# Statistic sums once a round behind a branch, a store's two issues apart, and fourteen steps loaded at once, in a displaced 5x5 convolution kernel

## The reference

```python
def _gn(v, G=32, eps=1e-5):
    g = v.reshape(B_, G, C_ // G, H_, W_)
    return ((g - mean(g)) / jnp.sqrt(var(g) + eps)).reshape(v.shape)
...
off_round = jnp.round(offset)                 # offset: [48, 2]
disp = _displace(x, off_round.astype(int32))  # shifted, zeros from outside
d = field[None] + (offset - off_round)[:, None, None, :]
kernel = jnp.exp(-jnp.sum(d * d, axis=-1) / (2.0 * SIGMA ** 2))
kernel = kernel / jnp.sum(kernel, axis=(1, 2), keepdims=True)
out = lax.conv_general_dilated(disp, kw, padding=[(2, 2), (2, 2)], feature_group_count=C)
...
x = x + _L0_conv_ref(_gn(x), L0_conv_offset)
```

## Time and profile before

| | |
|---|---|
| median of three runs | 1189.24 us |
| profiled execution: its own time / its span | 1188.73 us / 1186.6 us |
| TensorE busy (matmul / weight load) | 96% / 95% |
| VectorE, GpSimd, ScalarE busy | 81%, 72%, 63% |
| granted TensorE clock, mean | 0.997 |
| DMA traffic | 403 MB, 340 GB/s over the span |

### The profile page before, as it was taken

The page is one execution under the profiler, slowest core; times in us unless marked ns, Lnnn a source line. Parts: engine busy times, 40 slices in busy tenths (PEclk is TensorE's granted clock), DMA queues, the critical chain, the costliest instruction groups (busy, mean ns, idle before and its releaser), DMA issues. The chain is left out here.

```text
span 1186.6 us, 113109 instructions
## 1 busy us (share of the span) xinstructions
PE 1142.1 (96%) x50608; PEld 1123.1 (95%) x50608; DVE 966.9 (81%) x1373; ACT 752.5 (63%) x874; POOL 851.0 (72%) x1176
## 2 busy tenths in 40 slices
PE   7799999999999999999999999999999999999998
PEld 7799999999999999999999999999999999999998
DVE  8588878888888888888888888878888788888872
ACT  4466666666666666666666666666666666666663
POOL 7477777777776867867777776866867777776863
PEclk9999999999999999999999999999999999999998
DMA  9399999999999999999999999999999999999966
GB/s 310 106 381 356 350 359 346 358 356 348 349 360 348 349 352 353 351 358 350 358 356 336 354 361 351 348 357 343 358 348 353 354 348 356 350 349 363 354 233 212
DMA packets 409763, 402.99 MB, mean 340 GB/s; under 512 B 16528, under 2 KB 409744, under 8 KB 409744
## 3 DMA queue, kind: packets, MB, share of 16 engines
q1 hardware_dynamic: 206544, 202.98, 51.3%
q10 hardware_dynamic: 203200, 199.79, 49.7%
HBM read 201.38 MB, written 201.33 MB: 339 GB/s over the span
## 5 line engine op out<-in xcount | busy, mean ns | idle before, releaser
L755 PE MATMUL ps<-ay,norm 32*128 32x128 f32 x24768 | 746.8, 274 | 5.5 <-ACTq L729 3.7
L755 PEld LDWEIGHTS ps<-ay,norm 32*128 32x128 f32 x24768 | 718.1, 188 | 10.6 <-issue 6.3
L656 ACT ACTIVATE y<-ps 128x1152 f32<-128x1152 f32 (+1 forms) x256 | 309.9, 1211 | 291.4 <-PE ps L742 158.7
L507 DVE BATCH_NORM_STATS2 stats<-xin 128x6 f32<-128x512 f32 x768 | 482.8, 694 | 3.7 <-DMA xin<-in_x_dram 3.5
L767 PEld LDWEIGHTS ps<-ax,y 64*64 64x64 f32 x24576 | 376.1, 135 | 46.1 <-issue 40.7
L767 PE MATMUL ps<-ax,y 64*64 64x64 f32 x24576 | 386.1, 219 | 32.7 <-ACT x L673 16.3
L538 DVE TENSOR_TENSOR xin<-ps,xin 128x1024 f32<-128x1024 f32 x256 | 313.5, 1225 | 95.4 <-PE ps L767 93.1
L337 POOL TENSOR_TENSOR xin<-x,xin 128x512 f32<-128x512 f32 x256 | 321.4, 1277 | 7.8 <-ACT x L673 7.4
L346 POOL TENSOR_SCALAR norm<-xin,rstd,bias 128x768 f32<-128x768 f32 x256 | 251.9, 987 | 72.4 <-issue 49.0
L645 ACT ACTIVATE norm<-xin,bias,rstd 128x768 f32<-128x768 f32 x256 | 260.7, 1018 | 0.6 <-POOL bias L331 0.6
L673 ACT ACTIVATE x<-ps 128x512 f32<-128x512 f32 x256 | 148.4, 591 | 98.1 <-PE ps L767 81.8
(11 more groups left out here) (63 smaller groups left out, 216.1 us busy)
## 6 DMA issues: line engine op xcount, KB each, us to landing
xin<-in_x_dram SPq DMA_DIRECT2D x512, 384.0 KB, 6.1
out_dram<-xin ACTq DMA_DIRECT2D x508, 384.0 KB, 6.6
out_dram<-xin SPq DMA_DIRECT2D x4, 384.0 KB, 3.9
off<-in_L_conv_offset_dram SPq DMA_DIRECT2D x1, 48.0 KB, 3.2
```

The costliest lines, as they stand in the source:

```text
L507: nc.vector.bn_stats(stats[:, s // QUAD % 2, s % QUAD, n, :], xin[:, s].rearrange("p (g q) f -> p q f g", g=GROUPS)[:, n]).then_inc(bn_don ...
L656: nc.scalar.activation(y[:, j].rearrange("p k r a m -> p a (k r) m")[:, 0:lanes], ps[:, j % 2, 0:lanes, 0:POS * P].rearrange("p a (n m) -> ...
L755: last = nc.tensor.matmul(ps[:, v, a, P * k:P * (k + 1)], norm[rows, v, r, P * k:P * (k + 1)], ay[rows, k, r, :], start=(r == 0), stop=(r ...
```

## The change

It has three parts, and the bookkeeping of semaphores that they need.

1. `sum_stats` stands behind `pe.If(number > one)`, so only the second pair of a round takes the sums. The last row product of an even step now raises `y_done` itself, and the sums raise `stat_summed`. GpSimd's `make_summands` waits for `stat_summed` in place of `y_done`, and ScalarE's `copy_y` of step 2 waits for `stat_summed` too.
2. Step 3's store is split. Its first image is issued where both were; its second image is issued behind the first `copy_third`.
3. Fourteen steps are loaded at once, and the last two wait for `x_done` to reach 8 (all column products of the first round).

```diff
-FIRST = 12
+FIRST = 14
...
                 if s == FIRST:
-                    sync.wait_ge(y_done, QUAD + 1)
+                    sync.wait_ge(x_done, ADDS * QUAD)
...
-                    if first:
-                        pool.wait_ge(stat_summed, 2)
-                    else:
-                        pool.wait_ge(y_done, QUAD * (quad - 1) + 1)
+                    pool.wait_ge(stat_summed, quad + 1)
...
-                            dve.wait_ge(summands_ready, QUAD * quad + 2)
+                            dve.wait_ge(summands_ready, QUAD * quad)
...
-            def copy_y(t, j, first):
+            def copy_y(t, j, first, summed=None):
                 act.wait_ge(y_done, t + 1)
+                if summed is not None:
+                    act.wait_ge(stat_summed, summed)
...
-                copy_y(t + 2, 2, first)
+                copy_y(t + 2, 2, first, quad + 3)
                 store_of_last_round(2)
                 copy_y(t + 3, 3, first)
-                store_of_last_round(3)
+                store_of_last_round(3, (0,))
...
                 copy_third(t, s, first)
+                store_of_last_round(3, (1,))
                 copy_third(t + 1, s + 1, first)
...
-                if early is None:
-                    last.then_inc(y_done, 1)
-                else:
-                    last.then_inc(stat_summed, 1)
+                last.then_inc(stat_summed, 1)
...
-                y_product(2, 0, ends=early is not None)
+                y_product(2, 0, ends=True)
...
                 y_even(number)
-                pe.wait_ge(summands_ready, number)
-                sum_stats(0)
+                with pe.If(number > one):
+                    pe.wait_ge(summands_ready, one)
+                    sum_stats(0)
```

More of the change, by code:

```diff
@@ L279, in column_matrices, with make_summands @@
                                    ALU.mult).then_inc(ax_ready, STEPS)
-            def make_summands(quad, v, early=None, first=False):
+            def make_summands(quad, v, early=None):
                 part = slice(0, QUAD) if early is None else slice(PAIR * early, PAIR * (early + 1))
@@ L375, in one_round @@
                 else:
-                    make_summands(quad + 1, (g + 1) % 2, first=first)
-                    if first:
-                        pool.sem_inc(summands_ready, 2)
+                    make_summands(quad + 1, (g + 1) % 2)
                     coefficients(quad + 1, (g + 1) % 2, used=not first)
@@ L673, in copy_third, with store @@
                 nc.scalar.activation(x2[:, s % QUAD], ps[:, s % 2, 2:4, 0:ROW], ACT.Copy).then_inc(x2_ready, 1)
-            def store(c, s, t, images=B):
+            def store(c, s, t, images=(0, 1)):
                 act.wait_ge(result0_ready, t + 1)
                 act.wait_ge(result1_ready, SPARE + t + 1)
-                for b in range(images):
+                for b in images:
                     act.dma_start(out_t[s, b, c], xin[b:P:B, s]).then_inc(stored[s], 16)
@@ L683, in one_round, with store_of_last_round @@
                 group_follows = c is not NSUPER - 1
-                def store_of_last_round(j):
+                def store_of_last_round(j, images=(0, 1)):
                     if not first:
-                        store(c if g else c - 1, (s - QUAD + j) % STEPS, t - QUAD + j)
+                        store(c if g else c - 1, (s - QUAD + j) % STEPS, t - QUAD + j, images)
                 if group_follows:
@@ L718, in one_round @@
                 if last:
-                    store(c, s, t, images=1)
+                    store(c, s, t, images=(0,))
                 else:
@@ L724, in one_round @@
                     for j in range(1, QUAD):
-                        store(c, s + j, t + j, images=1)
+                        store(c, s + j, t + j, images=(0,))
             run(one_round)
@@ L847, in _ @@
             y_even(3)
-            pe.wait_ge(summands_ready, 3)
+            pe.wait_ge(summands_ready, 1)
             sum_stats(0)
```

## The result

The changed kernel takes 1162.43 us, the median of four runs (1160.82 to 1163.14), against 1189.97 (1188.84 to 1191.94) for the kernel before on the same chip. The ratio is 0.9765, interval 0.9747 to 0.9783. It is faster by 27.5 us. The forecast was 46 us, and the time is 2.4 us outside the predicted range. The profiled execution has a span of 1160.4 us and took 1162.17.

A forecast was written before the change was run, and what follows sets the result against it. TensorE's chain of matmuls and its pauses bound the kernel. Span 1186.6 - 16.6 (sums) - 29 (pauses) - 2.4 (start) + 2 (DMA) = 1140.6 us, forecast 1143 us, eight-in-ten range 1129 to 1160.

The forecast's parts named there:

- The pauses ahead of step 2: TensorE's column products wait for `copy_third` behind two store issues; splitting them saves 32 us (30 to 38), 3 back, net 29.
- Rival 1: Second store issue delays the second `copy_third`, so half of the 32 us returns ahead of step 3: 1156 us, chance 0.15.
- The sums: 64 of 130 `sum_stats` calls on TensorE go, at 0.26 us each: 16.6 us saved, bounds 11 and 24.
- The branches: Two new TensorE branches a pass cost nothing, being hidden; at worst 0.1 us a pass, 127 passes, 13 us.
- rival 3: Uncovered branch over the sums makes TensorE fetch code again, 1.7 us a round at the row products: 1252 us, chance 0.04.
- What is late next when the sum goes?: Next pair's row products need ScalarE's `normalise`; its slack shrinks from about 0.35 to 0.25 us and holds, costing nothing.
- the covers of part 2: First store issue, `copy_third` and VectorE's `add_x` end inside 2.81 us less 0.15, so the pause goes wholly.
- Part 3: Loading fourteen steps at once removes TensorE's 2.42 us loss at 62.33: 2.4 us saved; longer burst nothing, or 1 us either way.
- The DMA engines: Faster rounds need 371 GB/s; 382 over 30 us shows it fits, with 2 us charged for longer issues elsewhere.
- rival 2: Loads and stores cannot hold more than about 358 to 360 GB/s in steady rounds: 1168 us, chance 0.07.

The follow-up runs named there:

- part 2 alone: Changed kernel with sums twice a round without a branch and twelve steps loaded first, leaving only the split store: 1164.85 us, ratio 0.9798.
- two moves that empty GpSimd's chain: Changed kernel plus eight instructions; at block borders ScalarE's first store goes behind `normalise` and GpSimd's `add_third` behind `make_summands`: 1155.29 us.
- the unrolled kernel: Changed kernel with a round's two pairs written out on TensorE, no inner loop or branch, sums still once a round: 1764.91 us, ratio 1.4906.
- the padded kernel: Changed kernel with two small idle matmuls (eight instructions) ahead of TensorE's warm-up: 1155.31 us, ratio 0.9713.
- the run with shorter stores: Changed kernel with ScalarE's stores leaving out the last of six channel blocks: 1163.91 us, ratio 0.9797.
- the kernel with the late add: Changed kernel plus eight instructions; at block borders ScalarE's first store is behind `normalise` and GpSimd's `add_third` behind `make_summands`: 1155.29 us, ratio 0.9706.

## Why the prediction was wrong

The direction was right (0.94 for faster). Of the gain of 46 us, 27.5 came. Step by step:

- **The pauses ahead of step 2** (-32, bounds 30 to 38, 3 back): right in mechanism and size. 31.3 us went, named the right queue, and the part alone shows it (1164.85). One row was misread on the way: the 373 GB/s of the earlier trace rows begin at 617.56, when the pair of issues (615.81 to 617.84) was nearly over; in the window 615.56:617.56 the trace has 345. Why that pair took 2.03 us is open. Rival 1, a stall ahead of step 3, didn't happen: no piece of 384 breaks.
- **The sums** (-16.6 at 0.26): the mechanism was right and the term too large. 0.21 us a sum, 12.8 in the 61 rounds, inside the bounds of 11 to 24. I had called 0.255 "at most" and then taken it; the measured value lies midway between it and the 0.17 from start to start.
- **The branches** ("so nothing; at worst 0.1 us a pass"): this step failed. I looked for the cost where the branches stand, and there it is nothing: 288 records in one piece of 8.35 us. It appeared at the head of the loop over the rounds, whose gap of 0.32 us I had taken as fixed. The measured price is 0.155 us a round, 9.4 us. That is less than my "at worst" of 13 us, but neither the sum nor the range had a term for it. It comes with part 1; that it comes from the branch, and not from the sum that is no longer there or the other semaphores, is argued and not shown: no run has the branch and both sums. My rival 3 was the same kind of cost, "issue" in each round, but at the row products, and priced at 1.7 us a fetch. No code is fetched here (8 packets in both), and the price is an eleventh of it.
- **"What is late next when the sum goes?"** and the covers of part 2: this step failed too. I followed TensorE, ScalarE and VectorE through an ordinary round. The rounds in which a block begins have 1.0 us more on GpSimd ahead of its adds, and there the next late thing is ScalarE's store behind GpSimd's add. 15 rounds by 0.6 us is 9.0 us. The kernel with part 2 alone has them without any change to the sums, and two moves that empty GpSimd's chain remove them.
- **Part 3** (-2.4): wrong. The wait at 62.33 went, but the start of the profiled run was 0.85 us longer. The longer load burst ran until 36 us, just when the first pass fetches code, as windows of the kernel after show:

```profile
34.00:36.00 2.00, 2.00 (x78) 1.95 (x70) 0.92 (x2) 0.98 (x1) 0.38 (x1) 1.00 0.57 189
36.00:38.50 2.50, 0.14 (x6) 0.13 (x1) 1.07 (x2) 1.13 (x1) 2.18 (x6) 1.00 0.05 13
38.50:42.00 3.50, 2.60 (x127) 2.42 (x127) 1.23 (x1) 0.60 (x1) 3.18 (x5) 0.69 0.02 5
42.00:46.00 4.00, 3.69 (x127) 3.50 (x127) 1.22 (x1) 1.51 (x2) 2.13 (x2) 0.50 0.02 4
```

  TensorE stood for 2.4 us from 36.14 to 38.51, and then the granted clock was 0.69, a mean of both levels, and 0.50, which is 1.2 GHz. In the kernel before it was 1.00 there, and TensorE was busy for 2.00 of the 2.5 us from 36 on. That the longer burst delays the code is seen in the queue for instructions. Its third packet, by the times the code at the loop's head, starts between 32.6 and 33.9 us in the six kernels with twelve steps first, whose bursts end by 33.1, and between 34.6 and 36.1 in the twelve kernels with fourteen (here at 36.1), whose bursts end at 36.3 to 37.8; the second packet starts at 28.6 to 30.5 in both. What this is worth is less clear: the third round's column products start at 77.0 to 79.6 us with twelve and, the unrolled kernel left out, at 78.8 to 82.5 with fourteen, one profile of each. And the clock isn't tied to it: with twelve steps first it also fell (0.81 from 42 to 46), with no loads in 34 to 36, and in the padded kernel with fourteen it stayed at 1.00. I had priced all this as "nothing, or 1 us either way".
- **The DMA engines** (+2, rival 2 with 0.07): no term of the changed kernel, as the run with shorter stores shows (1163.91). So rival 2's 1168 us lie nearer to the measured time than the forecast only by luck. But the limit I had dismissed with 382 GB/s over 30 us exists in the faster kernels: loads and stores together held them at 361 to 364, and 371 were needed for my 16.96. With the hole and the border pauses gone, the kernel with the late add stopped at 1155 us, so the forecast's 1143 was out of reach by that alone. The row I chose was too short: the page of the kernel with the late add (GB/s in 40 slices of 29 us) has up to 380, and the same kernel holds 363 over 500 us:

```profile
GB/s 308 160 342 347 375 366 354 371 355 366 350 376 365 350 371 351 375 368 356 364 355 367 348 380 361 355 372 349 373 367 357 362 354 368 357 372 363 356 269 219
```

  The Trainium skill ("HBM Reference", Specifications (TRN2)) gives about 358 GB/s as a core's share when both cores of a pair stream, and about 425 for a core alone, as here; the measured 361 to 364, of loads and stores together, lie near the first and well below the second.

The span was forecast at 1140.6. Sums +3.8, pauses -2.3 (31.3 gone instead of 29 net), the head of the loop +9.4, border rounds +9.0, the start +3.2 (0.85 longer, not 2.4 shorter), the charge for the DMA engines -2.0 and the end of the kernel -1.4 make 1160.3, against 1160.4 measured.

Still open: why part 1 brings 0.28 us between the first LDWEIGHTS and the first MATMUL of a round, where it is 0.04 or 0.17 without part 1 and 0.02 to 0.04 with eight more instructions ahead of the loop. The runs show that eight instructions remove it and one doesn't. What the sequencer does in that time no record shows.

## What to carry to other kernels

When a pause goes, go through the round with the most work on each other engine, not through an ordinary one: the pause may have been covering it, and in the trace it carries the name of another engine. Look for the price of a branch in a hardware loop at the loop's head too, and run the change once more with eight instructions ahead of the loop before judging it. And take the rate that the rounds must hold from a stretch of many rounds: 30 us show more than 500 us hold.

## What the runs showed of the hardware that I had not expected

- Eight idle instructions ahead of a loop made it 7 us faster (1155.31 against 1162.43), through the gap at the loop's head: 0.48 us a round without them, 0.23 with them.
- A TensorE loop of some 1200 instructions fetched no code after its first pass. One of some 1560 fetched 281 packets more, 4.6 MB, stood for up to 11.2 us at a time, and took 1.49 times as long as the kernel before.
- On this core loads and stores of 1 KB rows held 361 to 364 GB/s over some 500 us however the pauses lay, though single slices of 29 us reached 380.
- A load burst longer by two steps (1.5 MB) made the third piece of TensorE's code start at 34.6 to 36.1 us and no longer at 32.6 to 33.9.
- A loop over a register range was passed once although its end was not above its start.
